# A selective-scan block on one core: gates, C weights and the softplus sum on GpSimd, both norms on ScalarE, and x and dt loaded into rings of their own

## The reference, cut to what matters

```python
xz = x @ W_in;  xh, z = split(xz)                  # x is layer-normed first
xc = depthwise_conv3x3(xh)
dt_r, B, C = split(xc @ W_xproj)
dt  = softplus(dt_r @ W_dt + b_dt)                 # 512 channels
dB  = (dt @ W_dtN + b_dtN) * B                     # 16 states
def step(h, t):                                    # 48*48 = 2304 steps, one after the other
    h = exp(dt_t[:, :, None] * A) * h + dB[:, None, :] * x_t[:, :, None]
    return h, einsum('bdn,bn->bd', h, C_t) + Dskip * x_t
y = layernorm(y) * ln_g + ln_b
y = y * silu(z)
x = x + (y @ W_out + b_out)
t = layernorm(x);  x = x + ffn(t)                  # a small exact table computation on 64 channels
```

## Time and profile before

| | before |
|---|---|
| median of 3 runs | 4375.35 us (4368.41 to 4375.43) |
| the profiled execution | 4363.87 us, its span 4362.1 us |
| DVE busy | 3931.4 us (90%) |
| PE busy | 3367.6 us (77%) |
| POOL busy | 2815.9 us (65%) |
| ACT busy | 2803.7 us (64%) |
| DMA, share of 16 engines | 78.0% in the queue that SP issues to |

### The profile page before, as it was taken

How to read it: one execution, slowest core, us unless ns; L and a number is a source line. 1 busy time by engine, 2 the same in 40 slices (tenths; PEclk the granted TensorE clock), 3 DMA queues, 4 the chain that set the end, 5 groups by cost and what they waited for, 6 DMA issues and landing times.

```text
span 4362.1 us, 101858 instructions
## 1 busy us (share of the span) xinstructions
PE 3367.6 (77%) x33792; PEld 1637.9 (38%) x33792; DVE 3931.4 (90%) x13181; ACT 2803.7 (64%) x5762; POOL 2815.9 (65%) x5195
## 2 busy tenths in 40 slices
PE   5778787878787877777787878787878777777765
PEld 2334333433343334333343334333433343333322
DVE  2899999999999999999999999999999999999998
ACT  2666666666666666666666666666666666666654
POOL 0766666666666666666666666666666666666664
PEclk8778887888778878888888878887888788878776
DMA  3878788878888787878787878788888788787875
GB/s 73 201 184 191 182 187 184 189 184 186 184 192 184 186 187 183 190 180 194 181 193 179 190 183 192 178 188 185 189 186 185 181 188 188 182 189 180 187 165 116
DMA packets 300438, 790.14 MB, mean 181 GB/s; under 512 B 71301, under 2 KB 225926, under 8 KB 226182
## 3 DMA queue, kind: packets, MB, share of 16 engines
q1 hardware_dynamic: 299910, 783.62, 78.0%
HBM read 648.18 MB, written 96.73 MB: 171 GB/s over the span
## 4 chain that ended last, share of the span: by engine, by line
DVE 42%; PE 35%; ACT 11%; issue 6%; DMA 3%; SPq 2%; POOL 1%; ACTq 0%; POOLq 0%; DVEq 0%
PE ps_s L508 7%; DVE h L843 7%; PE ps_y L472 6%; DVE ps_a L827 6%; PE ps_s L563 5%; DVE h L846 5%; DVE ps_a L830 4%; ACT ps_a L618 4%; PE ps_y L456 3%; DMA xb<-xd 3%; DVE yn L915 3%; PE ps_s L517 3%; DVE dt L883 3%; PE ps_s L546 3%; PE ps_s L491 2%
## 5 line engine op out<-in xcount | busy, mean ns | idle before, releaser
L618 ACT ACTIVATE ps_a<-xb,a_n 128x384 f32<-128x384 f32 x2304 | 1247.0, 574 | 988.1 <-DVE h L846 973.5
L1150 POOL TENSOR_TENSOR mp<-ap,h 128x128 f32<-128x128 f32 x2304 | 1120.0, 486 | 544.6 <-ACT ap L628 407.9
L1160 POOL TENSOR_TENSOR h<-mp,up 128x128 f32<-128x128 f32 x2304 | 1090.6, 473 | 475.3 <-PE ps_y L472 293.0
L1140 POOL TENSOR_TENSOR up<-xb,db 128x512 f32<-128x512 f32 x576 | 627.5, 1089 | 486.3 <-DMA xb<-xd 408.5
L846 DVE SCALAR_TENSOR_TENSOR h<-xb,db,ps_a 128x192 f32<-128x192 f32 x2304 | 926.1, 402 | 0.0
L843 DVE SCALAR_TENSOR_TENSOR h<-xb,db,ps_a 128x192 f32<-128x192 f32 x2304 | 920.2, 399 | 2.2 <-PE ps_y L472 0.6
L472 PE MATMUL ps_y<-h,cw 64*32 64x256 f32 x18432 | 806.6, 470 | 93.5 <-DVE h L846 92.7
L827 DVE TENSOR_TENSOR ps_a<-ps_a,h 128x192 f32<-128x192 f32 x2304 | 810.3, 352 | 29.2 <-ACT ps_a L618 26.6
L830 DVE TENSOR_TENSOR ps_a<-ps_a,h 128x192 f32<-128x192 f32 x2304 | 805.6, 350 | 0.0
L628 ACT ACTIVATE ap<-xb,a_n 128x256 f32<-128x256 f32 x1152 | 519.1, 500 | 198.1 <-DMA xb<-xd 196.8
L472 PEld LDWEIGHTS ps_y<-h,cw 64*32 64x32 f32 x18432 | 319.7, 124 | 531.0 <-issue 322.3
(11 more groups left out here) (109 smaller groups left out, 4038.9 us busy)
## 6 DMA issues: line engine op xcount, KB each, us to landing
xb<-xd SPq DMA_DIRECT2D x576, 1024.0 KB, 7.9
xs<-xh SPq DMA_DIRECT2D x196, 192.0 KB, 8.6
xd<-dttok SPq DMA_DIRECT2D x288, 128.0 KB, 6.0
xin<-in_x_dram SPq DMA_DIRECT2D x144, 128.0 KB, 7.0
xd<-xtok SPq DMA_DIRECT2D x192, 96.0 KB
res<-in_x_dram SPq DMA_DIRECT2D x144, 128.0 KB, 7.1
out_dram<-res SPq DMA_DIRECT2D x144, 128.0 KB, 6.8
xd<-xtok SPq DMA_DIRECT2D x192, 64.0 KB
```

The lines of the kernel that those rows point to most:

```text
L618: ins = act.activation(ps_a[buf][:, n, 0:2 * VD].rearrange("p (t d) -> p t d", t=2), xb[:, u % XUNITS, 2 * buf:2 * buf + 2, 1, 0:VD], ACT.Exp,
L1140: pool.tensor_tensor(up[:, Q % 2], x4, db4.broadcast_to([P, 4, 2, VP]), ALU.mult).then_inc(u_ready, 1)
L1150: pool.tensor_tensor(mp[:, G % 2], ap[:, Q % 2, G % 4], h[:, (G - 1) % HRING, :, VD:HALF], ALU.mult) \
L1160: pool.tensor_tensor(h[:, G % HRING, :, VD:HALF], mp[:, G % 2], up[:, Q % 2, G % 4], ALU.add) \
```

## The change

- POOL instead of DVE: `finish_dt` (now two operations of 768 columns in slots 16 and 17), `gate_y` (slots 21 to 24), `weigh_c` (same slots). In POOL's list they stand behind the two operations of the step of that slot.
- ACT instead of DVE: `y_norm` (slots 14, 15, 16) and `ln1_apply` (slots 23, 26, 28), as Identity with a scale and a bias for each partition. DVE only forms the bias, one operation on 128x3 each (`y_shift_by` slot 10, `ln1_shift_by` slot 19).
- x and dt lie in two DRAM buffers and are loaded by two DMAs, 4 KB for each partition each, into rings of their own: four units for x, three for dt. dt's unit comes free when ACT is done with it, x's when DVE and POOL are.
- Slots: x's transposes move ahead of y's (14, 15, 16 against 18 to 21); the output projection 29, 30, 31; `make_db` at 28; `add_residual` 30, 31, 32; the second norm and the table computation later by one or two slots, its last two additions in slot 0 of the next iteration; in SP's list the store of the output at 6, `bounce_states` at 30, `load_states` at 34.
- tanh is written into the y buffer `yn`, so `th` is gone; this adds waits of `gate_tanh` for `out_done` and of `scale_yn` for `sz_ready`.

The diff, cut to its core:

```diff
-XUNITS = 3
+XUNITS, DUNITS = 4, 3
 XLN_ROWS = 4
 SLOT = {
-    "conv": (0, 1, 3, 4), "xproj": (6,), "dtp": (8, 9, 11, 12), "yt": (14, 15, 16, 18), "xtok": (19, 20, 21),
-    "dttok": (23, 24, 26), "dtn": (27,), "out": (28, 30, 31), "z": (33, 34, 36, 37), "xlnT": (39, 40),
+    "conv": (0, 1, 3, 4), "xproj": (6,), "dtp": (8, 9, 11, 12), "xtok": (14, 15, 16), "yt": (18, 19, 20, 21),
+    "dttok": (23, 24, 26), "dtn": (27,), "out": (29, 30, 31), "z": (33, 34, 36, 37), "xlnT": (39, 40),
     "proj": (42, 43, 45, 46),
...
-        xb = sb("xb", [P, XUNITS, 4, 2, HALF])
+        xb = sb("xb", [P, XUNITS, 4, HALF])
+        dtb = sb("dtb", [P, DUNITS, 4, HALF])
...
             def load_x(r, k):
-
                 u = r * QUADS + k
                 if k == 0:
                     sp.wait_ge(x_stored, (r + 1) * 2 * len(X_PARTS) * SEM_DMA)
-                    sp.wait_ge(dt_stored, (r + 1) * 2 * KT * SEM_DMA)
                 if u >= XUNITS:
                     sp.wait_ge(h_ready, 4 * (u - XUNITS + 1))
                     sp.wait_ge(u_ready, u - XUNITS + 1)
-                src = xd[r % 2, :, :, 4 * k:4 * k + 4].rearrange("c b w s d -> (c b) (w s d)").unsqueeze(1)
-                sp.dma_start(xb[:, u % XUNITS], src.broadcast_to([2 * IMAGES, 8, 4 * DI])) \
-                  .then_inc(x_loaded[u % XUNITS], SEM_DMA)
+                sp.dma_start(xb[:, u % XUNITS], spread(0, r, k)).then_inc(x_loaded[u % XUNITS], SEM_DMA)
+
+            def load_dt(r, k):
+                u = r * QUADS + k
+                if k == 0:
+                    sp.wait_ge(dt_stored, (r + 1) * 2 * KT * SEM_DMA)
+                if u >= DUNITS:
+                    sp.wait_ge(a_ready, 2 * (u - DUNITS + 1))
+                    sp.wait_ge(ap_ready, u - DUNITS + 1)
+                sp.dma_start(dtb[:, u % DUNITS], spread(1, r, k)).then_inc(dt_loaded[u % DUNITS], SEM_DMA)
...
                     if s % 4 == 0:
-                        k = s // 4 + 2
+                        k = s // 4 + DUNITS - 1
+                        if k < QUADS and exists(i):
+                            load_dt(i, k)
+                        if k >= QUADS and exists(i + 1):
+                            load_dt(i + 1, k - QUADS)
...
+            def ln1_apply(r, k):
+                if k == 0:
+                    act.wait_ge(ln1_shift, r + 1)
+                    act.wait_ge(ln1_rstd, r + 1)
+                act.activation(xin[:, k, :], xin[:, k, :], ACT.Identity, bias=nm1[:, k:k + 1],
+                               scale=rs1[:, k:k + 1]).then_inc(xln_ready, 1)
+
+            def y_norm(r, k):
+                if k == 0:
+                    act.wait_ge(y_shift, r + 1)
+                    act.wait_ge(y_rstd, r + 1)
+                act.activation(y[:, k, :], y[:, k, :], ACT.Identity, bias=nmy[:, k:k + 1],
+                               scale=rsy[:, k:k + 1]).then_inc(y_normed, 1)
...
+                if g == 0:
+                    act.wait_ge(sz_ready, r * NG + NG)
...
                 n = r * NG + g
+                if r >= 1 and g == 0:
+                    act.wait_ge(out_done, r * KT)
                 if n >= 2:
                     act.wait_ge(sz_ready, n - 1)
-                act.activation(th[:, n % 2, :], shared_bank("z", r, g)[:, 0:TOK], ACT.Tanh, scale=0.5) \
+                act.activation(yn[:, n % 2, :], shared_bank("z", r, g)[:, 0:TOK], ACT.Tanh, scale=0.5) \
                    .then_inc(th_ready, 1)
...
+            def ln1_shift_by(r):
+                dve.wait_ge(ln1_rstd, r + 1)
+                if r >= 1:
+                    dve.wait_ge(xln_ready, r * KT)
+                dve.scalar_tensor_tensor(nm1[:], mv1[:, :, 0], -1.0, rs1[:], ALU.mult, ALU.mult).then_inc(ln1_shift, 1)
...
+            def y_shift_by(r):
+                dve.wait_ge(y_rstd, r + 1)
+                if r >= 1:
+                    dve.wait_ge(y_normed, r * KT)
+                dve.scalar_tensor_tensor(nmy[:], mvy[:, :, 0], -1.0, rsy[:], ALU.mult, ALU.mult).then_inc(y_shift, 1)
...
+            def weigh_c(third):
+
+                r, k = third // KT, third % KT
+                if k == 0:
+                    pool.wait_ge(states_loaded, (r + 1) * 4 * SEM_DMA)
+                if third >= 2:
+                    pool.wait_ge(c_done, 4 * (third - 1))
+                for n in range(2):
+                    dst = cw[:, third % 2, n, :, 0:P].rearrange("p q (j f) -> p q j f", f=32)[:, :, :, 0:IMAGES]
+                    c = cs[:, r % 2, n, k * THIRD:(k + 1) * THIRD].rearrange("p (q j) -> p q j", j=4)
+                    ins = pool.tensor_tensor(dst, c.unsqueeze(3).broadcast_to([P, 4, 4, IMAGES]),
+                                             mod8[:].unsqueeze(1).unsqueeze(1).broadcast_to([P, 4, 4, IMAGES]), ALU.mult)
+                ins.then_inc(cw_ready, 1)
+
+            def finish_dt(r, half):
+                pool.wait_ge(sp_log, r * 2 + half + 1)
+                part = dt[:, 2 * half:2 * half + 2, :].rearrange("p g t -> p (g t)")
+                pool.tensor_tensor(part, part, dttok[:, 2 * half * TOK:(2 * half + 2) * TOK], ALU.add).then_inc(dt_ready, 1)
+
+            def gate_y(r, g):
+                pool.wait_ge(yn_ready, r * NG + g + 1)
+                pool.wait_ge(sz_ready, r * NG + g + 1)
+                pool.tensor_tensor(yn[:, g, :], yn[:, g, :], sz[:, g, :], ALU.mult).then_inc(gated, 1)
...
+            for i in range(-1, LAST_ROW + 1):
+                for s in range(SIDE):
+                    G = SIDE * i + s
+                    if exists(i):
+                        if s % 4 == 0:
+                            pool_input(G // 4)
+                        pool_decay(G)
+                        pool_add(G)
+                    if s in (16, 17) and exists(i + 1):
+                        finish_dt(i + 1, s - 16)
+                    if s in (10, 27) and exists(i):
+                        weigh_c(i * KT + s // 16 + 1)
+                    if s == 43 and exists(i + 1):
+                        weigh_c((i + 1) * KT)
+                    if s in (21, 22, 23, 24) and exists(i - 1):
+                        gate_y(i - 1, s - 21)
```

More of the change, by code:

```diff
@@ L216, in build @@
         x_loaded = [sem(f"x_loaded{n}") for n in range(XUNITS)]
+        dt_loaded = [sem(f"dt_loaded{n}") for n in range(DUNITS)]
         m0_done = sem("m0_done")
@@ L347, in store_x @@
                     for half in range(2):
-                        steps = xd[r % 2, half, :, :, 0, :].rearrange("b (q j) d -> j q b d", j=4)[j]
+                        steps = xd[r % 2, 0, half].rearrange("b (q j) d -> j q b d", j=4)[j]
                         sp.dma_start(steps[q0:q0 + n // IMAGES], xtok[lo:lo + n, k, half * HALF:(half + 1) * HALF]) \
@@ L354, in store_dt, with spread @@
                 if r >= 2:
-                    for n in range(XUNITS):
-                        sp.wait_ge(x_loaded[n], (r - 1) * (QUADS // XUNITS) * SEM_DMA)
+                    for n in range(DUNITS):
+                        sp.wait_ge(dt_loaded[n], (r - 1) * (QUADS // DUNITS) * SEM_DMA)
                 for k in range(KT):
                     for half in range(2):
-                        sp.dma_start(xd[r % 2, half, :, 16 * k:16 * k + 16, 1, :].rearrange("b w d -> w b d"),
+                        sp.dma_start(xd[r % 2, 1, half, :, 16 * k:16 * k + 16, :].rearrange("b w d -> w b d"),
                                      dttok[:, k * DI + half * HALF:k * DI + (half + 1) * HALF]) \
                           .then_inc(dt_stored, SEM_DMA)
+            def spread(which, r, k):
+                src = xd[r % 2, which, :, :, 4 * k:4 * k + 4].rearrange("c b w d -> (c b) (w d)").unsqueeze(1)
+                return src.broadcast_to([2 * IMAGES, 8, 4 * HALF])
             def load_x(r, k):
@@ L418, in _ @@
                             load_x(i + 1, k - QUADS)
-                    if s == 2 and exists(i - 2):
+                    if s == 6 and exists(i - 2):
                         store(i - 2)
@@ L428, in _ @@
                         store_dt(i + 1)
-                    if s == 28 and exists(i + 1):
+                    if s == 30 and exists(i + 1):
                         bounce_states(i + 1)
-                    if s == 32 and exists(i + 1):
+                    if s == 34 and exists(i + 1):
                         load_states(i + 1)
@@ L627, in decay_pool @@
                 for n in range(2):
-                    ins = act.activation(ap[:, Q % 2, :, n, :], xb[:, Q % XUNITS, :, 1, VD:HALF], ACT.Exp,
+                    ins = act.activation(ap[:, Q % 2, :, n, :], dtb[:, Q % DUNITS, :, VD:HALF], ACT.Exp,
                                          scale=a_n[:, n:n + 1])
@@ L790, in _ @@
                             y_scale(i - 1)
+                        if s in (14, 15, 16):
+                            y_norm(i - 1, s - 14)
                         if s - 1 in SLOT["yt"]:
@@ L807, in _ @@
                             ln1_scale(i + 4)
+                        if s in (23, 26, 28):
+                            ln1_apply(i + 4, (23, 26, 28).index(s))
```

(25 more changed lines are left out.)

97 lines of the change are left out of this document (37 added, 60 removed).

## The result

The changed kernel takes 4008.36 us in the median of four runs (4006.37 to 4022.24) against 4375.39 for the kernel before, measured beside it: a ratio of 0.917, with a 95% interval of 0.915 to 0.919. The forecast was 4010.

What follows compares the result with a forecast made beforehand. DVE was taken as the bound, 87.8 us a row; -8.8 - 4.5 + 4.5 + 0.7 + 0.5 = -7.6 gives 80.2, times 48 -365 us: 3999 profiled, 4010 median; this case spans 3850 to 4180.

Steps and rivals of the forecast that it cites:

- Work off DVE: On DVE: gates, softplus sum, y_norm, C weights and first norm leave, 432.4 us in all, 9.0 a row.
- The two 128x3 operations: On DVE: the new bias operations cost about 0.1 us each, 0.2 a row, bounds 0 and 0.25.
- "Port": POOL shares SBUF interfaces with DVE and contends with its two-SBUF-input or two-port instructions; gate 716 ns against make_sz 542.
- Waits that go: On DVE: waits of y_norm (2.4), make_db (1.15) and second norm (1.0) vanish, together 4.5 us a row.
- The output projection's wait: DVE's residual waiting for PE's output projection: 1.9 us a row stays and grows by 0.7.
- The new wait for ACT: DVE waits for ACT's `ps_a` in slots 8 to 27: 4.5 us a row, bounds 1 and 8.
- POOL: Moved work adds 10.5 us a row to POOL, 75 in all, and costs nothing in the forecast.
- Rings: DMA and SP: twice the DMAs lengthen SP's list, a loss of 0.5 us a row, between 0 and 2.
- The first: Rival: DVE's new waits hardly appear because ACT keeps up; -11.8 us a row, 3810 us, chance 0.12.
- The second: Rival: POOL becomes the bound at 83.5 us a row, 4170 us, chance 0.24.
- The third: Rival: on the DMA queue, 4 KB pieces cost as much as 8 KB ones; slower, 5960 us, chance 0.05.
- The fourth: Rival: the work moved off DVE was hidden already, so the time stays the same; chance 0.03.

Runs made afterwards that it cites:

- e6: Changed kernel with the two 128x3 DVE operations each split into three one-column operations with one SBUF tensor: 4012 us, ratio 0.920 to the kernel before.
- e7: Changed kernel with all moved work back on DVE, so only slots and rings are new: 4211 us, ratio 0.964 to the kernel before.
- e3: Changed kernel with one extra unused 384-column ACT operation behind each y_norm, slots 14 to 16: 4086 us, ratio 0.934 to the kernel before.
- e1: Changed kernel with y_norm and the first norm back on DVE, the two 128x3 operations gone: 3926 us, ratio 0.898 to the kernel before.
- f3: e1 with one extra unused 384-column ACT operation in each of slots 14, 15, 16: 4001 us, ratio 0.916 to the kernel before.
- e2: Changed kernel with only the first norm back on DVE (slots 20 to 22), its 128x3 operation gone: 4002 us, ratio 0.916 to the kernel before.
- e8: Changed kernel with four ring units for dt and three for x: 3999 us, ratio 0.916 to the kernel before.
- e4: Changed kernel with one extra unused 384-column POOL operation in each of slots 1 to 4: 4089 us, ratio 0.936 to the kernel before.
- e5: Changed kernel with x and dt again in one load and one ring of three units: 4084 us, ratio 0.935 to the kernel before.
- f4: e1 with y_norm one slot earlier on DVE (12 to 14): 3918 us, ratio 0.896 to the kernel before.
- f1: e1 with four ring units for dt and three for x: 3931 us, ratio 0.900 to the kernel before.

## Why the prediction was right, step by step

The mechanism held: DVE shed work, the waits at the moved slots went, and a wait for ACT took the place of some of it. The row was met within 0.5 us. Several terms were not; they cancelled. DVE's busy time and its waits fill its span, so the two profiled executions (4362.1 and 4020.4 us) can be compared term by term, in us a row (terms rounded):

| | forecast | measured |
|---|---|---|
| DVE's work | -8.8 | -6.4 |
| waits of y_norm, make_db, second norm | -4.5 | -4.1 |
| wait for ACT in `ps_a` | +4.5 | +4.4 |
| wait for the residual | +0.7 | -1.2 |
| rings, and all other waits | +0.5 | +0.3 |
| sum | -7.6 | -7.1 |

- **Work off DVE**, 9.0 us a row: all of it left DVE's list. But its busy time fell by 309 us, not 420, because what stayed grew, next.
- **The two 128x3 operations**, 0.2 a row: wrong, 1.8. This is the term "cost about 0.1 us each", with bounds of 0 and 0.25. They take 1000 and 806 ns (L934 and L907), (48.0 + 38.7)/48 = 1.8 us a row, because they wait for POOL's instruction (e6). "No row shows this form" was wrong as well: the trace of the kernel before has it in the table computation, with a mean above the upper bound:

```profile
L966 DVE SCALAR_TENSOR_TENSOR amp<-amp,hot 128x3 f32<-128x3 f32 x48 | 16.4, 342 | 0.0
```

Single ones took 148 to 379 ns, and the 41 of 48 that started during a POOL instruction ended 0.02 us after it, there too. Other operations on SBUF lasted longer than before too, next to POOL's instructions; by line in the changed kernel:

```profile
L976 DVE TENSOR_SCALAR res<-res,sc 128x256 f32<-128x256 f32 x144 | 64.5, 500 | 0.0
...
L934 DVE SCALAR_TENSOR_TENSOR nmy<-mvy,rsy 128x3 f32<-128x3 f32 x48 | 48.0, 1000 | 12.0 <-ACT rsy L732 12.0
L978 DVE TENSOR_SCALAR hot<-hot 128x192 f32<-128x192 f32 x48 | 40.5, 843 | 0.0
...
L907 DVE SCALAR_TENSOR_TENSOR nm<-mv,rs 128x3 f32<-128x3 f32 x48 | 38.7, 806 | 25.5 <-ACT rs L708 25.5
L1027 DVE TENSOR_TENSOR res<-res,hots 128x48 f32<-128x48 f32 x48 | 36.8, 768 | 0.1
```

Before, L978, L1027 and L992 (not shown, 706 ns now) lasted 247, 258 and 187 ns, together 78 us more now. All 46 of L978 that started during a POOL instruction ended 0.11 to 0.12 us after it; POOL's instruction of 1.06 us stood beside 29 of them, and a C weight, which POOL has only since the change, beside 16. L976, the first of these rows, won 30 us instead. The prediction knew the shared interface ("Port") and took it for an effect on the gates alone. The rule of the Trainium skill (GPSIMD Engine Reference, section 1, Specifications) named the mechanism; the traces agree and show its size, which is the rest of POOL's instruction.
- **Waits that go**, 4.5 a row: right, 4.1. e7 shows that slots and rings do it, without moved work.
- **The output projection's wait**, 1.9 staying and 0.7 added: wrong. It fell to 34.8 us, 0.7 a row, a difference of 1.9 against the step. e7 has it too (37.7), so it isn't the moved work. The step counted PE's 2.55 us for each part against DVE's two steps. It left out that the first residual now stands one slot behind the first output projection (30 against 29), where before it stood one ahead (27 against 28). That this is the reason is read from the slots; no run moved these alone.
- **The new wait for ACT**, 4.5 a row: right in size, 4.9 measured, 4.4 more than before. The norms on ACT were dearer than taken, 831 and 617 ns:

```profile
L721 ACT ACTIVATE y<-y,nmy,rsy 128x512 f32<-128x512 f32 x144 | 119.5, 831 | 0.2 <-DVE nmy L934 0.2
...
L714 ACT ACTIVATE xin<-xin,nm,rs 128x256 f32<-128x256 f32 x144 | 88.3, 617 | 2.4 <-DVE nm L907 2.4
```

e3, e1 and f3 confirm ACT as the limit. The place was too wide: slots 14 to 18 (e2), not 8 to 27. Part of the wait, about 1 us before slot 32, goes when dt comes earlier (e8) and also when the first norm leaves ACT (e2); either way the time gains under 10 us.
- **POOL**, 10.5 us a row and nothing on the path: 481.1 us or 10.0 a row, by line:

```profile
L1169 POOL TENSOR_TENSOR h<-mp,up 128x128 f32<-128x128 f32 x2304 | 1052.5, 457 | 357.6 <-PE ps_y L492 147.4 <-POOL mp L1159 74.3
...
L1194 POOL TENSOR_TENSOR yn<-yn,sz 128x384 f32<-128x384 f32 x192 | 192.6, 1004 | 16.1 <-ACT yn L771 16.1
L1189 POOL TENSOR_TENSOR dt<-dt,dttok 128x768 f32<-128x768 f32 x96 | 173.7, 1810 | 108.9 <-ACT dt L698 108.9
L1182 POOL TENSOR_TENSOR cw<-cs,mod 128x128 f32<-128x128 f32 x288 | 114.8, 418 | 17.5 <-DMA cs<-bounce 17.5
```

The sum of 768 columns took 1810 ns, above the taken 1.49 us and inside the bounds. My 10.5 is near. The estimate with the Trainium skill's 2.6 cycles an element (GPSIMD Engine Reference, section 3.1) was 11 us a row; the cycles alone give less, and the prediction doesn't show what else is in it. POOL's own two operations of a step fell from 486 and 473 to 457 ns, so its busy time stayed under the 3250 us that I had named. "Costs nothing" holds for the list, not for the interface: e4 shows that POOL's time beside DVE's operations on SBUF is paid by DVE.
- **Rings**, a loss of 0.5 a row: wrong in sign. e5 has them at a gain of 1.6. The step looked at SP's longer list, and it is longer (twice 12 loads), but not at what an earlier dt does for ACT, whose wait for the load it had called free. This gain has no line of its own in the table: without the rings the wait for ACT would be longer.
- **Rivals.** The first fell: ACT's wait came. The second fell as put, POOL isn't the bound. The third fell: the DMA work shrank by 302 us. It was the sign of a few per cent that mattered there, and it went the other way. The fourth fell with the 8.3%.

So two errors stand against each other, a row: +2.4 in DVE's work (+1.6 for the two 128x3 operations, (78 - 30)/48 = +1.0 for the other lines above) and -1.9 in the residual's wait. They come from different places, and that they cancel is luck. So is the last step to 2 us: the profiled execution came out at 4022, where the sum gave 3999, and the median was taken to lie 11.5 us above it and lay 14 below.

What stays open: what sets the chain when both DVE's and ACT's waits are small. In f4 DVE is busy 94%; 70 us of its waits are for ACT and 87 for PE, and the latter grew in e2, e8, f1 and f4 when something else was taken away. No run changed PE's stages. A kernel with less work on ACT in slots 14 to 16 than e1 wasn't tried either. PE's granted clock was also higher after the change, 0.854 in the profiled execution against 0.812; what this brought was not tested. Among f4's four runs it differed as much as 0.858 and 0.878, and these two took 3915 and 3922 us.
